# Graph network on one core: block 0's result rows finished among the gathers, dense units one per wave in the first 15 waves

## What is computed

```python
h = relu(layernorm(x))
x = x + spline_conv(h, edge_attr, src, dst)
h = relu(layernorm(x))
alpha = leaky_relu(a_src[src] + a_dst[dst])       # 8 heads, self loops added
out   = segment_sum(softmax(alpha over dst) * xp[src], dst).mean(heads) + bias
h2 = layernorm(out + h) * g1 + be1
x = x + layernorm(relu(h2 @ w1 + b1) @ w2 + b2 + h2) * g2 + be2
```

## Time and profile before

| | |
|---|---|
| median of 3 runs | 3327.99 us (3320.49 to 3328.42) |
| profiled execution | 3314.93 us |
| its span, first to last instruction | 3313.1 us |
| busy: PE, DVE, ACT, POOL | 68%, 56%, 25%, 77% of the span |
| mean granted TensorE clock | 0.785 |
| last gather of part D starts | 2517.8 us |
| scatters of results | 2634.8 to 3310.1 us |

### The profile page before, as it was taken

One profiled execution on the slowest core, in us unless ns is written; L12 is line 12 of the kernel. 1 busy time (PEld: TensorE's weight loads), 2 busy tenths in 40 slices (PEclk: granted clock), 3 DMA queues, 4 the chain that ended last, 5 costly groups with the idle time before them and its releaser, 6 DMA issues.

```text
span 3313.1 us, 33504 instructions
## 1 busy us (share of the span) xinstructions
PE 2241.8 (68%) x10666; PEld 1571.2 (47%) x10666; DVE 1858.4 (56%) x3250; ACT 841.2 (25%) x1614; POOL 2543.9 (77%) x2011
## 2 busy tenths in 40 slices
PE   2877777757777777777777645737767557888730
PEld 1554544535555655565555434534444334455420
DVE  4787988894443433434333313347767578989610
ACT  1332222212323232333323212322222212222210
POOL 7788888888787888788888788888883166888877
PEclk9888888877878787887777766767888668888755
DMA  2322232221212111212111111111110101111100
GB/s 58 87 67 67 68 73 69 55 65 26 39 29 39 38 39 32 43 38 42 36 36 29 28 12 31 24 18 28 21 24 9 44 16 23 33 29 32 28 10 10
DMA packets 116212, 123.93 MB, mean 37 GB/s; under 512 B 70726, under 2 KB 72747, under 8 KB 116070
## 3 DMA queue, kind: packets, MB, share of 16 engines
q0 software_dynamic: 64000, 30.57, 9.9%
q1 hardware_dynamic: 52070, 91.52, 8.7%
HBM read 59.51 MB, written 64.00 MB: 37 GB/s over the span
## 4 chain that ended last, share of the span: by engine, by line
POOL 62%; issue 18%; DVE 9%; PE 9%; ACT 1%; DMA 0%; POOLq 0%; DVEq 0%; ACTq 0%
POOL ring L428 38%; POOL x_table L450 15%; POOL out_rows L476 9%; DVE region L1591 2%; PE V L793 2%; PE C L544 2%; PE V L532 1%; DVE region L1583 1%; PE C L508 1%; DVE region L1262 1%; PE T L493 1%; DVE region L1573 1%; DVE var L1231 1%; PE C L538 1%; PE C L540 0%
## 5 line engine op out<-in xcount | busy, mean ns | idle before, releaser
L428 POOL DMA_INDIRECT ring<-in_x,index x800 | 1040.4, 1300 | 244.3 <-issue 244.0
L476 POOL DMA_INDIRECT out_rows<-ring,index_out x400 | 518.8, 1297 | 272.3 <-DVE ring L1403 152.0
L1231 DVE TENSOR_REDUCE var<-sq 125x16 f32<-125x512 f32 x325 | 220.8, 682 | 802.3 <-ACT sq L921 672.1
L428 POOL DMA_INDIRECT ring<-x_table,index x400 | 495.8, 1240 | 127.0 <-issue 127.0
L450 POOL DMA_INDIRECT x_table<-region,index_out x400 | 485.9, 1215 | 121.9 <-issue 121.9
L532 PE MATMUL V<-xT,w_q 128*128 128x500 f32 x600 | 363.3, 756 | 90.0 <-ACT hid L932 56.5
L921 ACT ACTIVATE sq<-C 125x512 f32<-125x512 f32 x300 | 179.2, 598 | 912.3 <-PE C L544 422.7
L544 PEld LDWEIGHTS C<-w_c,hid 128*125 128x125 f32 x2400 | 317.0, 217 | 0.0
L544 PE MATMUL C<-w_c,hid 128*125 128x32 f32 x2400 | 316.0, 295 | 0.0
L508 PE MATMUL C<-center,xT 128*125 128x128 f32 x1400 | 243.8, 333 | 104.6 <-DVE hrow L1253 61.7
L493 PE MATMUL T<-ident,hrow 125*128 125x125 f32 x1000 | 188.9, 326 | 167.6 <-DVE hrow L1247 137.0
(11 more groups left out here) (248 smaller groups left out, 3207.6 us busy)
## 6 DMA issues: line engine op xcount, KB each, us to landing
ring<-in_x,index POOLq DMA_INDIRECT x800
nodes<-in_x SPq DMA_DIRECT2D x25, 500.0 KB
x_table<-nodes SPq DMA_DIRECT2D x25, 500.0 KB
x_plain<-nodes SPq DMA_DIRECT2D x25, 500.0 KB
nodes<-x_plain SPq DMA_DIRECT2D x50, 250.0 KB
out_rows<-nodes SPq DMA_DIRECT2D x50, 250.0 KB
x_table<-region,index_out POOLq DMA_INDIRECT x400
ring<-x_table,index POOLq DMA_INDIRECT x400
```

The lines of the kernel that those rows point to most:

```text
L428: pool.indirect_dma_start(out=ring[0:P, j, s * F:(s + 1) * F], out_offset=None, in_=table, in_offset=bass.IndirectOffsetOnAxis(ap=index[0: ...
L476: pool.indirect_dma_start(out=out[:, :], out_offset=bass.IndirectOffsetOnAxis(ap=index_out[0:P, j, s:s + 1], axis=0), in_=ring[0:P, j, s * ...
L1231: v.tensor_reduce(unit(var, k), slots(squares(k)), AX.X, ALU.add).then_inc(var_ready, 1)
```

## The change

Part D becomes a function `d_wave(w)` with a table `wave(w)` of what is in a wave:

- dense units start one in each of waves 0 to 14, so their stages fill waves 0 to 16. They use four places in `nodes` instead of three.
- in waves 13 to 22 the values of blocks 0 and 1 stand between the wave's other steps, not behind them. ACT and PE split `hidden` in two halves.
- block 0's rows are summed and normalized in waves 18 to 22 (`y2`) and finished in 19 to 23 (`y3`); both blocks' carries are made in waves 18 and 23.
- part E starts with `y_second`, the former `y_first` with the rows of block 1, without the scan of block 1. Then follow `e_block(2, None)`, (3,2), (4,3), (None,4).
- finished rows go to the tile of differences (`diff`), not to `ring`; targets are read from `scatter_to`. `y_finish` neither waits for an earlier scatter nor copies indices. POOL's scatter loop is unrolled.
- SP loads the first three chunks of rows for the results in wave 11 and the other two in wave 16.

```diff
+D_SLOTS = (7, 8, 9, 6)
...
+Y_FROM = X_FROM + NJ
+FIRST_JOIN, SECOND_JOIN = (2, 3), (6, 7)
+X_END = (4, 5, 8, 9, 10)
...
+def wave(w):
+
+    at = {stage: w - lag for stage, lag in (("n3", 2), ("n2", 1), ("n1", 0)) if 0 <= w - lag < UD}
+    if X_FROM <= w < X_FROM + EARLY * NJ: at["x"] = w - X_FROM
+    if Y_FROM <= w < Y_FROM + NJ: at["y2"] = w - Y_FROM
+    if Y_FROM < w <= Y_FROM + NJ: at["y3"] = w - Y_FROM - 1
+    if w in (Y_FROM, Y_FROM + NJ): at["carry"] = (w - Y_FROM) // NJ
...
+                if w == X_FROM - 2:
+                    for k in range(NJ):
+                        sp.wait_ge(x1_saved[k], 16 * NB)
+                    for k in range(2):
+                        sp.wait_ge(base_saved[k], 16 * NB * (3 - k))
+                    all_stored(range(6))
+                    for k in range(3):
+                        e_load(k, k)
+                if w == UD + 1:
+                    all_stored(range(6, SLOTS))
+                    for k in range(3, NJ):
+                        e_load(k, k)
             with sp.Fori(0, NB - 1) as b:
                 for j in range(NJ):
...
+                pool.wait_ge(unit_out[k], 16 * LAST_TURN[k])
+            for c in range(NC):
+                pool.wait_ge(ring_filled, c + 1)
+                pool.sem_inc(cleared, 1)
+                for s in range(CE):
+                    e = c * CE + s
+                    pool.indirect_dma_start(
+                        out=out[:, :], out_offset=bass.IndirectOffsetOnAxis(ap=scatter_to[0:P, e:e + 1], axis=0),
+                        in_=diff[0:P, e * F:(e + 1) * F], in_offset=None,
+                        bounds_check=last_row, oob_is_err=False).then_inc(ring_dma[c % NJ], 16)
...
+            def d_wave(w):
+                at = wave(w)
+                b, j = divmod(w, NJ)
+                first, last, x = w == 0, w == NC, "x" in at
+                three = "n3" in at or "y3" in at
+                t = {}
+                if "n3" in at:
+                    pe.wait_ge(c_done, st["n2"] + 1 + CREDIT)
+                    t["n3"] = transpose(unit(hrow, 2))
+                if "y3" in at:
+                    t["n3"] = y_rows(0, at["y3"], 2)
+                if "n2" in at:
+                    pe.wait_ge(c_done, st["n1"] + 1 + CREDIT)
+                    t["n2"] = transpose(unit(hrow, 1))
+                if not first:
+                    pe.wait_ge(c_done, st["d1"] + 1 + CREDIT)
+                    t["d2"] = transpose(unit(hrow, 0))
+                if three:
+                    pe.wait_ge(t_done, t["n3"] + 1 + CREDIT)
+                    hidden(xT[:, 2, :], (0, 1))
+                if "n2" in at:
+                    st["n2"] = product(hT[:, 1, :], base_bd[:, :], bias=0, t_at=t["n2"])
+                if not first:
+                    product(hT[:, 0, :], src_bd[:, :, :].rearrange("f t h -> f (t h)"), n=4 * H, t_at=t["d2"])
+                if "carry" in at:
+                    x_tail_T(X_END[at["carry"]])
+                if three:
+                    hidden(xT[:, 2, :], (2, 3))
+                if not last:
+                    pe.wait_ge(ring_dma[j], (2 * NB + b + 1) * DMAS)
+                    t["d1"] = transpose(unit(ring, j))
+                if "n1" in at:
+                    u = at["n1"]
+                    pe.wait_ge(unit_in[slot_of(u)], 16 * turns_of(u))
+                    t["n1"] = transpose(place(slot_of(u)))
+                if "carry" in at:
+                    x_carry_T(X_END[at["carry"]])
+                if x:
+                    c, k = at["x"], EARLY_T[at["x"] % 2]
+                    if c == 0:
+                        pe.wait_ge(softmax_done, 1)
+                    t["x"] = transpose(diff[0:P, c * W:(c + 1) * W])
+                if not last:
+                    st["d1"] = product(xT[:, 0, :], center[:, :], t_at=t["d1"], frees=ring_used)
+                if x:
+                    open_sums(c)
+                    x_values(t["x"], k, 0, V)
+                if three:
+                    back_product(xT[:, 2, :])
+                if x: x_values(t["x"], k, 1, V)
+                if "n1" in at:
+                    st["n1"] = product(xT[:, 1, :], center[:, :], t_at=t["n1"])
+                if x:
+                    x_values(t["x"], k, 2, V)
+                    x_values(t["x"], k, 3, V)
...
+            def d_wave(w):
+                at = wave(w)
+                first, last = w == 0, w == NC
+                three = "n3" in at or "y3" in at
+                if three: affine()
+                if "n2" in at: evac(hT[:, 1, :])
+                if not first: evac(hT[:, 0, :])
+                if three: hidden((0, 1))
+                if "n2" in at: square(2)
+                if not first: cq.next()
+                if "carry" in at: x_tail_rows()
+                if three: hidden((2, 3))
+                if not last: evac(xT[:, 0, :])
+                if "n2" in at: root(2)
+                if "n1" in at: evac(xT[:, 1, :])
+                if "carry" in at: x_carry_rows()
+                if "x" in at: evac(hT[:, EARLY_T[at["x"] % 2], :])
+                if not last: square(0)
+                if "x" in at:
+                    cq.next()
+                    if not last: root(0)
+                if three: square(3)
+                if not last and "x" not in at: root(0)
+                if three: root(3)
+                if "n1" in at: square(1); root(1)
+                if "y2" in at: y_square(0, at["y2"]); root(2)
...
+            def d_wave(w):
+                at = wave(w)
+                b, j = divmod(w, NJ)
+                first, last, x = w == 0, w == NC, "x" in at
+                norm, pending = {}, []
+                if "n2" in at:
+                    norm["n2"] = spread(2)
+                    rows_over_std(2, norm["n2"])
+                if not first:
+                    dve.wait_ge(c_done, st["d1"] + 1 + CREDIT)
+                    logits_src(w - 1)
+                if not first and j == 0:
+                    ended = bass.ds((b - 1) * SE, SE)
+                    for h in range(H):
+                        i = v.tensor_tensor_scan(heads_of(self_logit)[:, h, ended], cont[0:P, ended], heads_of(beta)[:, h, ended], 0.0, ALU.mult, ALU.max)
+                    step(i)
+                if "carry" in at:
+                    x_carry(at["carry"])
+                if not last: norm["d1"] = spread(0)
+                if x: x_products(at["x"], 0, pending, V)
+                if "carry" in at and at["carry"] + 1 < EARLY:
+                    x_on(at["carry"])
+                if "y2" in at:
+                    if at["y2"] == 0:
+                        dve.wait_ge(rows_T, 2 * (X_END[0] - 2) + 2)
+                    y_sum(0, at["y2"])
+                if not last:
+                    relu_rows(0, norm["d1"])
+                    st["d1"] = cq.at
+                if x:
+                    at_c, rows = bank_ready()
+                    if at["x"] == 0:
+                        v.tensor_copy(open_sum, rows[0:H, 0:F]).then_inc(c_done, 1)
+                    else:
+                        v.tensor_tensor(open_sum, open_sum, rows[0:H, 0:F], ALU.add).then_inc(c_done, 1)
+                if "n3" in at or "y3" in at: norm["n3"] = spread(3)
+                if x: x_products(at["x"], 1, pending, V); x_sum(at["x"], pending)
+                if "n3" in at:
+                    rows = place(slot_of(at["n3"]))
+                    finish_rows(rows, rows, norm["n3"], unit_done)
+                if "y3" in at:
+                    y_finish(0, at["y3"], norm["n3"])
+                if "n1" in at: relu_rows(1, spread(1))
+                if "y2" in at: norm["y2"] = spread(2)
+                if x: x_products(at["x"], 2, pending, V); x_sum(at["x"], pending)
+                if "y2" in at: y_norm(2, norm["y2"])
+                if x:
+                    x_products(at["x"], 3, pending, V); x_sum(at["x"], pending); x_sum(at["x"], pending)
+                    if at["x"] % NJ == NJ - 1:
+                        x_tail(at["x"] // NJ)
...
             def y_finish(y, j, at):
 
-                dve.wait_ge(ring_dma[j], (3 * NB + y) * DMAS)
                 c = y * NJ + j
-                v.tensor_copy(index_out[0:P, j, :], scatter_to[0:P, c * CE:(c + 1) * CE])
-                finish_rows(nodes[0:P, j, 0:W], ring[0:P, j, :], at, ring_filled)
+                finish_rows(nodes[0:P, j, 0:W], diff[0:P, c * W:(c + 1) * W], at, ring_filled)
                 dve.wait_ge(ring_filled, c + 1)
                 dve.sem_inc(rows_used, 1)
...
-            for y in range(1, NB):
+            e_block(EARLY, None)
+            for y in range(EARLY, NB):
                 e_block(y + 1 if y + 1 < NB else None, y)
```

More of the change, by code:

```diff
@@ L48 @@
 UNIT_AT = (0, 1, 3, 4, 6, 7, 9)
[L49 to L52 removed]
+NU = len(UNIT_AT)
+SLOTS = 2 * NJ
+UD = NB * (SLOTS - NU)
+assert NB * SLOTS * CE == TN and UD + 2 <= NC
+D_SLOTS = (7, 8, 9, 6)
 CREDIT = 4
@@ L1004, in _ @@
                 b_turn(NB, turn(h, last=True))
```

(25 more changed lines are left out.)

387 lines of the change are left out of this document (133 added, 254 removed).

## The result

The change made the kernel slower by half a per cent: a median of 3340.63 us (20 runs, 3319.82 to 3354.68) against 3323.66 us for the kernel before (20 runs, 3306.66 to 3332.45) on the same chip, ratio 1.0049, 95% interval 1.0032 to 1.0065. I had forecast 3297 in a range up to 3326.

The account below looks back on a forecast made before the run. POOL was taken to carry 62% of the span, with spare time after 2518 us and none after 2807. Terms 41 - 21 + 77 - 127.5 = -30.5 us gave a median of 3297 us, range 3264 to 3326.

Parts of the forecast that it names:

- Step b: Waves 13 to 24, values interleaved and block 0's rows added: back product's wait not covered, 20 us later.
- R3: Rival: unhidden back product at lower TensorE clock, loop 86 us late, 3342 us; no gain beyond 71.5 late; chance 0.1.
- my forecast of 41: Loop's end: 41 us later, from 5 for dense waves, 16 for waves 10 and 11, 20 for interleaved waves.
- step a: Dense units one per wave in the first 15: loop 21 us later, 5 of lag and 16 at waves 10 and 11.
- R2: Rival: no change; dense waves take 27.5 us instead of 25, loop 70 us late, 3326 us; chance 0.16.
- Step c: Softmax stretch, now with block 1's rows: load wait goes, scan and its wait move into the waves, 21 us less.
- Step d: New stretch with values of block 2 and no rows: 77 us more.
- Step e: Scatters behind block 2's first finished rows: 15 groups and two scans in 376 us, 127.5 us less.

Follow-up runs that it names:

- e1: Changed kernel with VectorE's normalization of gathered rows moved ahead of the first value products and block 0's additions: 3295.69 us, ratio 0.9924.
- e8: e1 plus one value sum ahead of the back product's reduction and ScalarE's gathered-rows root ahead of the back product's square: 3266.39 us, ratio 0.9834.
- e5: Changed kernel with the hidden products undivided in waves without values: 3350.64 us, ratio 1.0076.
- e4: Kernel before with only the dense units moved, one per wave in the first 15, old instruction order, block 0's rows not in the loop: 3281.16 us, ratio 0.9876.
- e3: Changed kernel with all value work of a wave behind the back product and the unit's first product: 3286.17 us, ratio 0.9900.
- e10: e3 with ScalarE's root of the gathered rows ahead of the back product's square: 3278.65 us, ratio 0.9873.
- e9: Changed kernel with the back product's reduction ahead of the gathered rows' normalization in waves without values: 3330.86 us, ratio 1.0024.

## Why the prediction was wrong

**Step b is the one that failed, in a term of its chain.** I wrote the back product as done 5.5 us behind the normalization (10.3 to 15.8) and forecast +20; measured is 373.0 - 323.5 = +49.5. Put beside wave 19, counted from the end of the last sums at 2499.8: reduction of the gathered rows 5.5 (forecast 5.1), value products 7.7 (7.2), additions 9.8 (9.3), normalization 10.7 (10.3), and then the back product 21.1 against 15.8. Of these 5.3 us, 4.9 are that one duration, taken from wave 19 of before, where the granted clock was 1.00 and then 0.92. Here it was 0.50.

The 29.5 us that b is off by are made up so. My own sum of the waves was 347.5, and the waves took 373.0: 25.5 us. The other 4 come from setting the 347.5 against 327, measured from the end of the last join, where the same twelve waves of before took 323.5. Of the 25.5 us, the back product accounts for 13.0: in waves 19 to 22 it took 4.8, 1.7, 4.8 and 1.7 us more than 5.5. These waves came at 39.6, 36.4, 39.3 and 43.4 us against 33.3, 33.3, 33.3 and 40.5. (The terms listed for 33.3 add up to 32.9.) Another 8.4 lie in waves 13 and 14, 38.1 and 37.3 us against 33.5, and there the back product was not slow: 5.4 us in wave 13. In wave 13 DVE stands 2.2 us for the second stage's square at the wave's end, and then for its root:

```profile
2350.07 0.25 DVE L1272 RECIPROCAL rstd<-std 125x16 f32<-125x16 f32 x1 [2.69 <-ACT std L962]
```

On ScalarE that root now stands behind the second half of `hidden` and a copy. In wave 22 of before the wait for it was 0.44 us. No run here moves it. Wave 15 came out 3 us shorter than forecast, 16 to 18 about as forecast.

R3's mechanism, the clock falling behind an idle TensorE, is there in four of its nine waves, at 2 to 5 us each; in waves 13 to 16 and 23 the product was not slowed. Against R3 I had set that TensorE gets more work in these waves. That reading was wrong: it gets 56 matmuls fewer, and it stood idle just ahead of the product on which the wave hangs. e1 removes the cause by one move, and with it 45 of the 49.5 us.

**That R3's total fits is luck.** The loop is 90.4 us late where R3 had 86. Over my forecast of 41, 29.5 us come from step b, of which R3's own mechanism has 13 and not 45, 17.5 come from step a, and 2.3 from a later start.

**Step a is a second miss: 21 forecast, 38.5 measured** (15.8 in the first nine waves, 22.7 at the joins). The joins' part of 16 was right: with the root first, e8 needs 114.7 us there against 97.3, 17.4 more. The lag was not 5 but 16, plus 5 at the joins, and e8 takes 15 of these 21 away with one instruction of 0.3 us moved. My reason for 25 us a wave, that behind the split halves "the first product after them starts 2 us sooner", was aimed at the wrong engine. I looked at TensorE's order and passed over ScalarE's, where a root of 0.3 us stood behind a wait of 4.6 us. "The gathers don't notice" was wrong too: POOL stood 9.8 us for indices ahead of 2454.8, and the last gather started at 2531.9 instead of 2517.8. That cost nothing, since POOL has to wait for rows later on. R2's waves of 27.5 us were wrong as well: 25.3 to 26.7 on all but the first.

**Step c: -21 forecast, -15.3 measured** (144.9 us to the reset of the carry at 2831.4, against 160.2). **Step d: 77 forecast, 76.6 measured.** The first rows of block 2 took another 1.8 us over those of before. **Step e: 376 forecast, 376.0 measured**, and the wait of over 90 us between blocks 1 and 2 is 92.9; the groups of blocks 3 and 4 wait for nobody. The sum with measured sizes: 38.5 + 2.3 (wave 0 itself came 2.3 us later) + 49.5 - 15.3 + 76.6 + 1.8 - 127.4 = +26.0 us, against 26.1 between the two spans. The medians differ by 17.0; the spread of single executions, some 35 us for after, covers that.

**What of the idea stands.** Since 15 groups and two scans stand behind block 2's first rows in every version that has block 0's rows in the loop, each us in the loop's end is a us of the kernel: from the last logits to the end it takes 652 to 655 us in all of them but e5 (659). After ends its loop 90.4 us late, more than the 71.5 at which R3 said nothing is left. Put right (e8), it is worth 55 us. But e4 has 38 of these from the units' place alone. Block 0's rows in the loop and the mended orders add some 15 (ratios 0.9876 and 0.9834, intervals apart by a hair), and with e3's order (e10) nothing that can be told from e4. Counted from the first logits, the profiled executions took 1319.8 us in e4, 1310.6 in e8 and 1317.2 in e10, so 9 of the 15 are seen in the part that differs. Whether e4 would gain from the root moved as in e8 was not tried, so how much of the 15 is block 0's rows stays open.

## What to carry to other kernels

Where a producer is moved into a busy wave, follow the bank it writes: what frees it, what stands ahead of the freeing instruction in its engine's queue, and what the longest product costs if TensorE has stood just before it. Read the queues of TensorE, VectorE and ScalarE for a short instruction behind a long wait; here two such places, a normalization and a root, were worth 45 and 15 us of the loop. Price a move at both ends, what it burdens and what it frees.

## What was not expected of the hardware

Two runs of the same 42 matmuls took 5.4 us (e1) and 10.3 us (after, wave 19); what differs is 3.7 us of idle TensorE ahead and a granted clock of 1.00 in the one and 0.50 in the other. At 1.2 instead of 2.4 GHz the ratio would be 2; here it is 1.9. In wave 20 the same idle time stood ahead and L564 ran at 0.50 as well, but L570 then took 3.69 us at 0.95. In wave 21 of e9 4.0 us stood ahead, L564 still took 1.12 us at 1.00, and L570 6.76 at 0.50. So in these waves the lower level followed the pause each time, but when it set in and how long it stayed differed; what decides that, no run here tells.

A scatter that begins under a row of scans can stay on the engine until the scans have ended. In after, POOL and then DVE:

```profile
3004.74 1.19 POOL L502 DMA_INDIRECT out_rows<-region,scatter_to  x1 [0.30 <-issue]
3006.24 7.83 POOL L502 DMA_INDIRECT out_rows<-region,scatter_to  x1 [0.30 <-issue]
```

```profile
3005.29 0.67 DVE L1267 TENSOR_REDUCE var<-sq 125x16 f32<-125x512 f32 x1
3005.88 2.30 DVE L1298 TENSOR_TENSOR_SCAN region<-cont,region 125x80 f32<-125x80 f32 x10
```

(The last row's count and time are cut at the window's end; there are 32 scans in 7.1 us.) The scatter began 0.4 us after the first scan and took 7.83 us instead of 1.19. Three scatters are held so in after, for 6.26, 7.83 and 7.24 us, and each ends 1.1 us after the last scan. The Trainium skill's page "SBUF — State Buffer", section "SBUF: two separate sides", has the lock held for one instruction. By that alone a scatter could have gone in between two of the 32 scans, which these three did not. One did, though: ahead of the first of the three, POOL and then DVE,

```profile
2651.45 1.30 POOL L502 DMA_INDIRECT out_rows<-region,scatter_to  x1 [0.30 <-issue]
```

```profile
2651.15 7.11 DVE L1298 TENSOR_TENSOR_SCAN region<-cont,region 125x80 f32<-125x80 f32 x32
```

it began 0.3 us after the first scan and was done in 1.30 us; only the next one, at 2653.06, was held. What tells the two cases apart stays open. The two held scatters behind block 2's first rows cost 12.7 us together (7.83 and 7.24 less 1.19 each), where step e had kept 11.5.
